# A GRU scan on one core: TensorE's order of the parts of a step

## The reference

```python
def step(H, xs):
    xz, xr, xh = xs                       # x @ Wx*.T + bx*, for this step
    Z = sigmoid(xz + H @ Whz.T + bhz)
    R = sigmoid(xr + H @ Whr.T + bhr)
    H_tilda = tanh(xh + (R * H) @ Whh.T + bhh)
    H_new = Z * H + (1.0 - Z) * H_tilda
    Y = H_new @ Whq.T + bhq
    return (H_new, Y)
out = x + transpose(scan(step, cond, ...))
```

## Time and profile before

| | |
|---|---|
| median of 3 runs | 525.94 us (525.78 to 526.23) |
| the profiled execution | 528.27 us, span 526.5 us, TensorE's granted clock 0.993 |
| PE busy / PEld busy | 511.4 us (97%) / 493.9 us (94%) |
| DVE busy / ACT busy | 317.7 us (60%) / 329.6 us (63%) |
| matmul and weight load rows | 44212 each |
| mean HBM traffic | 53 GB/s |

### The profile page before, as it was taken

The page is one execution under the profiler, slowest core; times in us unless marked ns, Lnnn a source line. Parts: engine busy times, 40 slices in busy tenths (PEclk is TensorE's granted clock), DMA queues, the critical chain, the costliest instruction groups (busy, mean ns, idle before and its releaser), DMA issues.

```text
span 526.5 us, 96122 instructions
## 1 busy us (share of the span) xinstructions
PE 511.4 (97%) x44212; PEld 493.9 (94%) x44212; DVE 317.7 (60%) x1929; ACT 329.6 (63%) x1800; POOL 0.2 (0%) x4
## 2 busy tenths in 40 slices
PE   7499999999999999999999999999999999999997
PEld 7399999999999999999999999999999999999996
DVE  0246666666666666666666666666666666666664
ACT  2256666666666666666666666666666666666664
POOL 0000000000000000000000000000000000000000
PEclk9989999999999999999999999999999999999999
DMA  5011111111112111111111111111111111111111
GB/s 174 26 40 45 55 50 50 53 47 50 55 45 54 50 45 55 50 50 55 45 50 55 45 55 50 49 53 48 50 55 45 53 51 45 55 50 48 54 48 52
DMA packets 57881, 27.66 MB, mean 53 GB/s; under 512 B 6928, under 2 KB 56976, under 8 KB 57872
## 3 DMA queue, kind: packets, MB, share of 16 engines
q1 hardware_dynamic: 56736, 26.63, 18.0%
q10 hardware_dynamic: 1136, 0.89, 0.5%
HBM read 18.98 MB, written 8.52 MB: 52 GB/s over the span
## 4 chain that ended last, share of the span: by engine, by line
PE 97%; issue 2%; DMA 0%; DVE 0%; ACT 0%; SPq 0%; DVEq 0%; ACTq 0%
PE r_ps L241 34%; PE c_ps L241 28%; PE z_ps L241 23%; PE y_ps L241 11%; DMA xres_sb<-in_xr_dram 0%; DVE o_sb L209 0%; ACT c_ps L151 0%; SPq L126 0%; DVE u_sb L227 0%; ACT c_sb L186 0%; ACT r_ps L151 0%; ACT z_ps L151 0%; DVE ones_sb L197 0%; DVE h_sb L232 0%; SPq L127 0%
## 5 line engine op out<-in xcount | busy, mean ns | idle before, releaser
L241 PE MATMUL c_ps<-xt_sb,wx_sb 128*32 128x64 f32 x4128 | 173.5, 225 | 2.1 <-issue 2.1
L241 PE MATMUL z_ps<-xt_sb,wx_sb 128*32 128x64 f32 x4128 | 163.7, 221 | 2.2 <-issue 2.2
L176 ACT ACTIVATE r_sb<-r_ps 128x32 f32<-128x32 f32 x512 | 91.4, 198 | 109.1 <-PE r_ps L241 101.6
L222 DVE TENSOR_TENSOR rh_sb<-r_sb,h_sb 128x32 f32<-128x32 f32 x512 | 90.0, 192 | 85.1 <-ACT r_sb L176 81.0
L241 PE MATMUL z_ps<-h_sb,whz_sb 128*32 128x32 f32 x8192 | 124.5, 198 | 1.1 <-issue 1.1
L241 PE MATMUL c_ps<-rh_sb,whh_sb 128*32 128x32 f32 x8192 | 122.8, 198 | 0.0
L241 PE MATMUL y_ps<-whq_sb,h_sb 128*32 128x128 f32 x2064 | 113.6, 280 | 0.3 <-DVE h_sb L232 0.3
L241 PE MATMUL r_ps<-xt_sb,wx_sb 128*32 128x64 f32 x4128 | 107.8, 219 | 3.2 <-issue 1.9
L241 PEld LDWEIGHTS z_ps<-h_sb,whz_sb 128*32 128x32 f32 x8192 | 109.3, 111 | 1.3 <-issue 1.3
L227 DVE SCALAR_TENSOR_TENSOR u_sb<-z_sb,c_sb 128x32 f32<-128x32 f32 x512 | 75.3, 189 | 54.3 <-ACT c_sb L186 54.3
L241 PEld LDWEIGHTS z_ps<-xt_sb,wx_sb 128*32 128x32 f32 x4128 | 101.2, 111 | 2.3 <-issue 2.3
(11 more groups left out here) (27 smaller groups left out, 369.3 us busy)
## 6 DMA issues: line engine op xcount, KB each, us to landing
xt_sb<-in_xt_dram SPq DMA_DIRECT2D x130, 64.0 KB, 1.8
xres_sb<-in_xr_dram SPq DMA_DIRECT2D x130, 64.0 KB, 1.8
out_dram<-o_sb SPq DMA_DIRECT2D x130, 64.0 KB, 1.6
wx_sb<-in_wx_dram SPq DMA_DIRECT2D x2, 256.0 KB, 3.7
wx_sb<-in_wx_dram ACTq DMA_DIRECT2D x1, 256.0 KB, 4.3
whz_sb<-in_whz_dram SPq DMA_DIRECT2D x1, 256.0 KB, 4.6
whr_sb<-in_whr_dram ACTq DMA_DIRECT2D x1, 256.0 KB, 5.4
whq_sb<-in_whq_dram SPq DMA_DIRECT2D x1, 256.0 KB, 5.7
```

The costliest lines, as they stand in the source:

```text
L176: nc.scalar.activation(r_sb[:, o], r_ps[:, o, here], ACT.Sigmoid).then_inc(s_r[o], 1)
L222: nc.vector.tensor_tensor(rh_sb[:, k], r_sb[:, k], old[:, k], ALU.mult).then_inc(s_rh[k], 1)
L241: return nc.tensor.matmul(ps, weights, moving, start=start, stop=False, skip_group_check=True, **kw)
```

## The change

In TensorE's program the four z parts (and their wait for the second half of H) come directly behind the four r parts. The two x parts of the candidate follow them, in one run with the x part of the update gate. The y part moves, in steps 0 to 2, from the end of the step to the place between the last x part of the update gate and those of the reset gate, with its wait for the seed of y in steps 0 and 2; the parts from `zh` are then the last of the step. In step 3, before the jump, y stays last. On ScalarE the update sigmoid comes ahead of the seed of the reset gate. No instruction, wait or transfer is added or removed.

```diff
--- before.py
+++ after.py
@@ -174,10 +174,10 @@
                     for o in range(K):
                         act.wait_ge(s_r_ps[o], t + 1)
                         nc.scalar.activation(r_sb[:, o], r_ps[:, o, here], ACT.Sigmoid).then_inc(s_r[o], 1)
+                    act.wait_ge(s_z_ps, t + 1)
+                    nc.scalar.activation(z_sb[:], z_view(p)[:, :, B * s:B * s + B], ACT.Sigmoid).then_inc(s_z, 1)
                     if s == 0:
                         seed(r_ps[:, :, W * (1 - p):W * (1 - p) + W], R).then_inc(s_seed_r, CS)
-                    act.wait_ge(s_z_ps, t + 1)
-                    nc.scalar.activation(z_sb[:], z_view(p)[:, :, B * s:B * s + B], ACT.Sigmoid).then_inc(s_z, 1)
                     if s == CS - 1:
                         act.wait_ge(s_res, t + CS)
                         seed_y(p).then_inc(s_seed_y, CS)
@@ -262,6 +262,13 @@
                     last = mm(y_ps[p][B * j:B * j + B, 0, 0:P], h_sb[:, k, CS * p + step], whq_sb[:, k, P * half:P * half + P],
                               tile_position=(0, B * j))
                 return last
+
+            def y_step(t, q, s):
+                if s == 0:
+                    pe.wait_ge(s_seed_y, t + 1)
+                last = y_piece(q, s)
+                if s == CS - 1:
+                    last.then_inc(s_y_ps, 1)
 
             def r_part(u, k, o, moving):
                 return columns(r_ps[:, o], slice(B * u, B * u + B), whr_sb, k, o, moving)
@@ -317,16 +324,16 @@
                         pe.wait_ge(s_h[0], t + 1)
                         r_part(u, 0, 1, old[:, 0]).then_inc(s_r_ps[1], 1)
 
-                    if s == 0:
-                        pe.wait_ge(s_seed_c, t + 1)
-                    x_piece(q, N, pieces[0])
                     if u > 0:
                         pe.wait_ge(s_h[1], t + 1)
                     for o in range(K):
                         for k in range(K):
                             z_mm = columns(z_ps[p][:, 0], slice(W * o + B * s, W * o + B * s + B), whz_sb, k, o, old[:, k])
                     z_mm.then_inc(s_z_ps, 1)
-                    x_piece(q, N, pieces[1])
+                    if s == 0:
+                        pe.wait_ge(s_seed_c, t + 1)
+                    for piece in pieces:
+                        x_piece(q, N, piece)
                     if s == 0:
                         pe.wait_ge(s_seed_z, t + 1)
                     x_piece(q, Z, pieces[0])
@@ -339,6 +346,9 @@
                                 c_mm.then_inc(s_c_ps[o], 1)
 
                     x_piece(q, Z, pieces[1])
+
+                    if u < SLOTS - 1:
+                        y_step(t, q, s)
                     if s == 0:
                         pe.wait_ge(s_seed_r, t + 1)
                     for piece in pieces:
@@ -348,11 +358,8 @@
                     pe.wait_ge(s_zh, t + 1)
                     for k, o in AHEAD[(u + 1) % SLOTS]:
                         r_part((u + 1) % SLOTS, k, o, zh_sb[:, k])
-                    if s == 0:
-                        pe.wait_ge(s_seed_y, t + 1)
-                    y_mm = y_piece(q, s)
-                    if s == CS - 1:
-                        y_mm.then_inc(s_y_ps, 1)
+                    if u == SLOTS - 1:
+                        y_step(t, q, s)
 
             pe.wait_ge(s_seed_y, T + 1)
             for k in range(K):
```

## The result

The changed kernel takes 532.8 us (median of 4 runs, 532.3 to 533.5), the kernel before beside it 526.1 (4 runs). The ratio is 1.0118, with a 95% interval of 1.0104 to 1.0132. The forecast was 522.6, and the time lies outside the range of 518.3 to 528.9.

The account below looks back on a forecast made before the run. The step was taken as r phase 0.29, ring 0.73 (ScalarE and VectorE) and TensorE-bound tail 0.90, 1.92 us. With the other moves at 0, (c)'s 3 x 0.017 x 64 = 3.3 us came off 525.9: 522.6, range 518.3 to 528.9.

Parts of the forecast that it names:

- term (a): z directly behind r on TensorE: work between r and c unchanged, z up to 0.03 us late but hidden, cost 0.
- a slack of 0.03: Third c part waits for rh anyway; its two predecessors need 0.13 of the 0.16 us between the rh products.
- The tail: Stretch from the third c part's load to the next r matmul, bound by TensorE, to stay at 0.90 us.
- the ring: From the last r matmul's start to the third c load: 0.73 us, fixed by ScalarE and VectorE; TensorE's work inside 0.71.
- wrong altogether: Sign against the forecast: z's first load over 0.03 late and c stage at 0.25, or y costing more than 0.22.
- The wait for h: Wait for h's second half, moved up one x part: margin 0.01 us, z up to 0.03 late if r gets tighter.
- (b): z sigmoid ahead of the reset seed on ScalarE: y covers the later seed, cost 0; without y some 0.05.
- (c): y out from between zh and r: r takes 0.24 to 0.27 us instead of 0.29, gaining 0.017 a step.
- the sum's 3.3 us: Total gain forecast: 0.017 us in three steps of four over 64 rounds.
- Rival 3: Slower: the wait directly behind r delays quarters or signal in steps 1 and 3, 3.3 us, 529.2 us; chance of slower 0.27.
- Its own sign: In steps 1 and 3, the delay from r's last end to the second sigmoid rises from 0.06 to 0.09 us.
- The jump: Step 3 into step 0: TensorE waits for VectorE's u_sb before the first r load; this wait stays.

Follow-up runs that it names:

- TensorE alone: Loops of whole steps added behind the last work of the kernel before, no other engine working; with waits and signals 7.71 us a round in the order before, 7.91 changed.
- z alone: Against the kernel before, only TensorE's z parts moved directly behind the r parts; y and ScalarE's order as before: 532.9 us, ratio 1.0093.
- y alone: Against the kernel before, only y moved among the x parts in steps 0 to 2; z and ScalarE as before: 528.4 us, ratio 1.0010.
- z split: The changed kernel with one candidate x part between the two halves of z: 527.4 us, ratio 1.0013 to the kernel before.

## Why the prediction was wrong

The step that failed is term (a), "Cost 0". Its cover was read rightly, and its size too: a slack of 0.03 a step is 0.12 a round, and the kernel before is 0.11 above TensorE alone in the same order (7.82 and 7.71). Wrong was the sentence before it, that the work between r and c is unchanged when one x part changes its place. I added up parts by their columns and gave the signals on them no price. In the order before, with an x part directly behind r, all signals together cost TensorE alone 0.05 a round; in the changed order, with the whole of z behind r, 0.24, and its stream with waits and signals is 0.05 us longer each step, 0.20 a round. That is more than the 0.11 of slack: 0.09 comes through, 0.02 more is not explained, and 0.11 x 64 = 7 us is the loss.

The tail was mis-sized as well. The prediction kept it at 0.90, from the third c part's load to the next r matmul. As medians of the steps 1 of 35 rounds:

| us | before | z alone | y alone | changed |
|---|---|---|---|---|
| third c load behind the second rh product | 0.052 | 0.070 | 0.053 | 0.069 |
| tail | 0.896 | 0.905 | 0.906 | 0.913 |

So of the 0.034 that a step 1 lost, one half is TensorE's lateness behind the ring and comes with z, and the other half lies in the tail, where z and y's new place bring about 0.01 each.

Half of my own sign for "wrong altogether" appeared: the c stage fell to 0.25, TensorE itself bound there. The other half, z's first load late behind r, did not.

The other points, one by one:

- *What bounds it.* The ring was read rightly: 0.73 fixed, TensorE's work inside it 0.71. I drew from it that small losses are free, and held only the late h against the slack of 0.03.
- *The wait for h.* The second half of h ends at 340.26 and z's first load starts at 340.33, 0.07 later, where a load that does wait comes 0.05 behind VectorE. Hardly late, as forecast; and step 0, which has no such wait, has the same long z.
- *(b), ScalarE's order.* Right that y covers the seed; the price without the cover was 0.09 to 0.10 in two steps of four, twice my 0.05.
- *(c), y out from between zh and r.* Wrong. The last r matmul starts 0.28 after the first (340.09 to 340.37), before 0.29, not 0.24 to 0.27. The little that r gained did not help either: the second sigmoid starts at 340.49 + 0.36 - 0.20 = 340.65, 0.56 after the first r matmul, and before 0.55 (337.20 - 336.65). Of the sum's 3.3 us nothing came, and nothing stood against (a).
- *Rival 3* had the right sign, and at 529.2 about half the price, but another mechanism. Its own sign did appear: from r's last end to the second sigmoid are 0.08 in step 1 (340.65 - 340.37 - 0.20), before 0.06. But with z alone, where the wait for h stands directly behind r, it is 0.064 as a median of steps 1, and with y alone, where it doesn't, 0.081; the wait is not what does it. And with z split that wait still stands directly behind r, and nearly nothing is lost.
- *The jump.* As forecast in the rows: behind it the first r load starts 0.09 after u_sb's end (346.02 - 345.93), in the earlier trace rows 0.08. But I had called this a wait for VectorE, and a load that does wait comes 0.05 behind. From y's first matmul to the next r matmul are 0.40 in both kernels (334.29 to 334.69, 345.63 to 346.03), and 0.41 where TensorE runs alone, in either order with waits that were met long before (793.86 to 794.27, 867.55 to 867.96). The jump itself, with its register waits, takes this time.

What stays open: why the signals on r make a long run of 32-column parts behind them slower, and hardly an order with a 64-column part there, while signals on z parts in the same run add nothing (no kernel was run with r's signals alone changed, and the split order not with signals alone); what lengthens the tail by 0.01 with either move; and why two unused signals cost 2.5 us in the kernel before (where TensorE alone was not tried with them).

## What to carry to other kernels

Before taking a reordering of one engine's work as neutral, look for what hangs on the moved instructions: a signalling matmul that had wide matmuls behind it may cost more with a long run of narrow ones there. Two limits that lie close together hide only a loss smaller than their distance, and that distance can be measured by letting the one engine run the same order alone. A cover such as y ahead of the reset parts can be worth 11 us and be invisible in a comparison of whole kernels, so take each part of a change alone.

## What the hardware showed that I had not expected

- Matmuls of 24 and of 32 columns on a quarter take the same in a long run, 0.067 and 0.068 us a part, or 8.4 ns from matmul to matmul over the four quarters; 48 columns take 0.084. The Trainium skill (TensorE: Matmul & The Clock Gate, "Wait — 56ns, not 53.3ns?") says that from start to start there are never less than about 25 ns however few the columns are. A floor shows here as well, but over matmuls on separate quarters it is a third of that.
- Signals: the two of r cost TensorE alone 0.05 us a step with z behind them ((7.76 - 7.55) / 4), z's own nothing. Seven met waits a step against registers cost 0.11 and 0.14 a round in the two orders, 0.10 of it at the jump; against constants 0.01 in the changed order (7.56 - 7.55).
- Only TensorE at work, a loop's first round took 16 to 20 us where nearly all later ones took 7.5 to 7.9, by a few gaps of 1 to 2.75 us.
